# Probabilities turned by DMA in every unit, the cache copied in three stages, and a new order of work on every engine

## Chip, cores and metric

The kernel runs on one core of one Trainium2 chip. The time is in microseconds (us) of the device; lower is better. A core has five engines that each work through their own list of instructions and wait for one another by semaphores: PE (TensorE, matrix products), DVE (VectorE), ACT (ScalarE), POOL (GpSimd) and SP (SyncE, which here only issues transfers). Sixteen DMA engines carry the transfers.

## The reference

Two steps, each added to x, which is 8 batches of 128 rows of 512 columns:

```python
x = x + einsum('bsi,boi->bso', x, lora_weight[adapter_ids])        # layer 0
q, k, v = x @ Wq.T, x @ Wk.T, x @ Wv.T                              # 32 query heads, 8 key heads, D = 128
q, k = rope(rmsnorm(q)), rope(rmsnorm(k))                           # k over 8 key heads
k_all = concat(k_cache[block_table], k); v_all = concat(v_cache[block_table], v)   # 512 + 128 keys
o = softmax(where(valid, q @ k_all.T * SCALE, -1e30)) @ v_all       # 4 query heads share a key head
x = x + o @ Wo.T
```

The cache has 64 pages of 32 rows, and each batch names 16 of them.

## The kernel before, in words

The work is 64 units: key head hk = u // 8, batch b = u % 8. A unit projects q (four heads), k and v, norms and rotates them, takes four blocks of scores of 128x640, turns them into probabilities, multiplies them by the values, and multiplies the result by Wo into a sum kept per batch. For accuracy every factor is split into a high and a low part in 16 bits, and each product is three products (`three`, L1655 to L1657): high by high, high by low, low by high. The splitting of weights, keys, values, outputs and probabilities is what fills DVE, ACT and POOL.

Every engine has its order written out by hand, in a loop over i. In period i, PE takes the scores of unit i (`scores`, L1729, results in S), projects unit j = i + 1 (Q and KV), multiplies the probabilities of unit w = i - 1 by the values (`times_v`, results in O) and projects the output of unit o = i - 2 (`project_o`, Y). DVE takes the row maxima (`largest`, L1331), each of which lets PE start the next block of scores. In the first periods PE also makes the products of layer 0 for batch i + 2 (`l0_product`, L1676) and turns x (`l0_turn`).

Probabilities must be turned (transposed) ahead of the product with the values. In units 0 to 7 (NA = 8) PE does that: DVE divides them by their sums (`norm`, L1255), PE turns them in five groups of four blocks (L1661, `turn_p`), ACT takes the high part (`p_hi`, L955) and DVE the low part (`p_lo`, L1365). From unit 8 on ACT writes a high plane (`upper_plane`, L1025), DVE a low plane (`lower_plane`, L1359), in pairs of heads, with the scale made by a two-column multiply (sm, L1344) and a reciprocal (rc, L1347); and SP issues four DMA transposes a unit (`turn_upper`, L535, and `turn_lower`, L547). Their results lie in the tiles `first` and `second`, which in the first periods hold the inputs of layer 0.

The cache is read in two ways. For units 0 to 8 (NL = 9) SP loads keys page by page (`load_kt`, L419, 16 transfers a unit) and POOL gathers values by row numbers (L636). The other heads' rows are copied in the first 14 periods to a block in device memory, `cache_rows`, in the order in which units want them: one transfer a page, 14 cache rows wide (12 for one batch), L427. `COPY_SP` and `COPY_ACT` say how many groups of four pages SP and ACT issue in each period. Later units load keys and values with one transfer each (`load_k`, L436, `load_v`, L522). In the loop of SP, `load_v` stands behind the copies of its period.

Weights of a head come in ten parts of 512 columns: 0 to 3 for q, 4 and 5 for k and v, 6 to 9 for the output. Each is loaded, squared (for a scale), its high part is made by ACT (L937) and its low part by POOL in two instructions (L647 scales it, L644 subtracts); the two 16-bit rings `wh` and `wl` have twenty places. The tables `SQUARES`, `HI_ACT`, `LO_POOL`, `LO_DVE` and `LOAD_AT` say in which period relative to a head's first unit each is done; parts 4 and 5 have both high and low part two periods ahead, and the projection of k and v for the head's first unit is done one period ahead.

Of the kernel before, what the change touches and what calls it, by code (L numbers as in the profile page):

```python
# [10 lines left out]
F16 = mybir.dt.float16  # L11
# [33 lines left out]
T_BANK = (0, 1, 0, 0, 1)  # L45

NL = NB + 1  # L50
NA = 8
# [8 lines left out]
QW_DOWN = 80.0 * ONE  # L60
ROOT_EPS = float(np.sqrt(D * EPS))
# [3 lines left out]
COPY_SP = (0, 1, 1, 1, 1, 1, 1, 2, 0, 1, 1, 1, 2, 0)  # L65
COPY_ACT = (2, 2, 3, 2, 2, 3, 3, 2, 1, 0, 0, 0, 0, 0)
NGRP = NPG // 4

# [8 lines left out]
LAST_SQUARES = {3: 0, 5: 1, 9: 2}  # L77
HI_ACT = {(0, 6): (1, 0), (0, 7): (1, 0), (0, 8): (1, 1), (0, 9): (1, 1),
# [5 lines left out]
LO_DVE = {(0, 6): (1, 1), (0, 7): (1, 1), (0, 9): (1, 1)}  # L84
LO_POOL = {(0, 8): (1, 1), (1, 0): (-4, 0), (1, 1): (-4, 1), (1, 2): (-3, 0), (1, 3): (-3, 1),
# [4 lines left out]
LOAD_AT = {(1, 0): -7, (1, 1): -7, (1, 2): -6, (1, 3): -6, (1, 4): -5, (1, 5): -5,  # L90
           (1, 6): -4, (1, 7): -3, (1, 8): -3, (1, 9): -2,
           0: -10, 1: -10, 2: -9, 3: -9, 4: -8, 5: -7, 6: -6, 7: -5, 8: -5, 9: -4}


def at_period(table, period, slot=None):

    found = []
    for hk in range(NK):
        for c in range(NWC):
            own = hk == 0 or (table is LO_POOL and (hk, c) in LO_DVE)  # L100
            if not ((hk, c) in table or (c in table and not own)):
                continue
            at = table[(hk, c)] if (hk, c) in table else table[c]
            if at == (period - NB * hk if slot is None else (period - NB * hk, slot)):
                found.append((hk, c))
    return found


def copies_of(period, act=False):


    if not 0 <= period < len(COPY_SP):
        return []
    first = sum(COPY_SP[:period]) + sum(COPY_ACT[:period]) + (COPY_SP[period] if act else 0)
    return [((k // NGRP + NL) % NB, k % NGRP)
            for k in range(first, first + (COPY_ACT if act else COPY_SP)[period])]


def build(nc, x, xt, lw, wall, kv, ids_lens, table, pages, qkw, consts, iota, out):
    with ExitStack() as ctx:  # L120
# [16 lines left out]
        wh = sb("wh", [P, 2 * NWC * WC], F16)  # L137
        wl = sb("wl", [P, 2 * NWC * WC], F16)
# [5 lines left out]
        mrow = sb("mrow", [NB, NT * P], BF16)  # L144
        iot = sb("iot", [NB, NT * P], F16)
# [19 lines left out]
        pth = sb("pth", [P, 3, G * P], F16)  # L165
        ptl = sb("ptl", [P, 3, G * P], F16)
        oh = sb("oh", [P, G * P], F16)
        ol = sb("ol", [P, G * P], F16)
        ones = sb("ones", [P, P], BF16)

# [21 lines left out]
        eq = sb("eq", [P, 2, NB])  # L192
        ek = sb("ek", [P, 2, NB])
# [23 lines left out]
        kidx1 = tabb[:, 0:NT * (NL - NB)]  # L217

# [3 lines left out]
        ang = pr[:, G * (NA % 2), 0:512].rearrange("p (b f) -> p b f", b=NB)  # L222
        rnd = pr[:, G * (NA % 2) + 1, 0:512].rearrange("p (b f) -> p b f", b=NB)
# [32 lines left out]
        def hi_made(hk, c):  # L256

            g = group(c)
            first_c, size = ((0, 4), (4, 2), (6, 4))[g]
            return size * hk + c - first_c + 1  # L260
# [8 lines left out]
        def plane(a):  # L269
            return a.bitcast(F16).rearrange("p (k n) -> p k n", n=P)  # L270

        planes = tuple((plane(f[:, 0:5 * HID // 2]), plane(f[:, 5 * HID // 2:5 * HID]))
                       for f in (first, second))
# [12 lines left out]
        def totals_at(m):  # L286
            return T[:, 0, 0:2] if m < 2 else KV[:, 384:386]

        def w_total_at(hk, g):
            if hk == 0 and g < 2:  # L290
# [21 lines left out]
        c_ilf, c_tabf, c_kidx, c_kidx1, c_pos, c_ang, c_sin, c_cos = (  # L312
            sem("c_ilf"), sem("c_tabf"), sem("c_kidx"), sem("c_kidx1"), sem("c_pos"), sem("c_ang"), sem("c_sin"),
# [7 lines left out]
        w_hi, w_lo = slots("w_hi", 3), slots("w_lo", 3)  # L321
# [4 lines left out]
        a_sqk, a_vn, a_sqq, a_exp, g_kh, a_kn, a_q, a_p, a_o = (  # L326
            sem("a_sqk"), sem("a_vn"), sem("a_sqq"), sem("a_exp"), sem("g_kh"), sem("a_kn"),
# [4 lines left out]
        made_vlo, g_kc, g_var, g_rst, v_prob = (  # L332
            sem("made_vlo"), sem("g_kc"), sem("g_var"), sem("g_rst"), sem("v_prob"))
# [3 lines left out]
        v_sm, a_f1, v_f2, g_qr = sem("v_sm"), sem("a_f1"), sem("v_f2"), sem("g_qr")  # L337
# [5 lines left out]
        w_sq, p_wt, v_ws, g_wr, g_wm = (slots("w_sq", 3), slots("p_wt", 3), slots("v_ws", 3),  # L343
                                        slots("g_wr", 3), sem("g_wm"))
# [3 lines left out]
        g_vm, g_km, v_vhi = sem("g_vm"), sem("g_km"), sem("v_vhi")  # L348
# [10 lines left out]
        copy_regs = [nc.scalar.alloc_register(f"copied{j}") for j in range(12)]  # L359
# [4 lines left out]
        def place(u):  # L364

            return (u - NA) % 2

        def slot(u, g):

            return G * place(u) + g if u < NA else (G * (u - NA) + g) % RING  # L370
# [7 lines left out]
        def turned_at(u, t):  # L378

            if u == LAST:  # L380
                return S[:, t - 2, :] if t in (2, 3) else T[:, t % 2, :]
            return T[:, T_BANK[t], :]

        def p_place(parts, u, t):

            if u == LAST:
                return planes[1][parts].rearrange("p k n -> p (k n)")[:, G * P * t:G * P * (t + 1)]
            return (pth, ptl)[parts][:, (5 * u + t) % 3, :]

        def turned_part(u, t):  # L390

            return 5 * (NA if u == LAST else u) + t
# [9 lines left out]
        def taken(u):  # L402

            return 16 * ((u - NA) // 2 + 1)
# [5 lines left out]
        def load_kt(e, regs, v, t):  # L410
            if v >= 3 and t == 0:
                e.wait_ge(g_kc, v - 2)
# [11 lines left out]
        def copy_page(e, b, k, number):  # L424

            rows = slice(2 if b >= NL - NB else 4, 2 * NK)
            e.dma_start(copy[rows, b, k, :].rearrange("r (s n) -> s r n", s=16),  # L427
                        kv[rows, bass.ds(number, 1), :].rearrange("r a (s n) -> (a s) r n", s=16)
                        ).then_inc(d_copy[b], 16)

        def load_k(e, v):
            hk, b = divmod(v, NB)
            if v < NL + NB:
                e.wait_ge(d_copy[b], 16 * NPG)
            e.wait_ge(g_kc, v - 2)
# [4 lines left out]
        def l0_bank(b):  # L440
            return Y[:, :] if b <= 3 else KV[:, :]

        def w_cols(hk, c):
            n = NWC * (hk % 2) + c
            return slice(n * WC, (n + 1) * WC)
# [4 lines left out]
        def wait_products(e, hk, c):  # L450

            if hk >= 2:
                u = NB * (hk - 1) - 1
                if c < 4:
                    e.wait_ge(p_q, 4 * u + c + 1)
                elif c < 6:
                    e.wait_ge(p_kv, u + 1)
                else:
                    e.wait_ge(p_y, 4 * u + c - 6 + 1)
# [19 lines left out]
        def _(e):  # L479
# [30 lines left out]
            def copy_pages(b, t):  # L510
# [3 lines left out]
                for j in range(4):  # L514
                    copy_page(e, b, 4 * t + j, numbers[j])

            def load_v(v):
                hk, b = divmod(v, NB)
                if v < NL + NB:
                    e.wait_ge(d_copy[b], 16 * NPG)  # L520
                e.wait_ge(made_vlo, v - 2)
# [4 lines left out]
            def turn_upper(u, pair):  # L526
                if pair == 0:


                    if u == NA:  # L530
                        e.wait_ge(l_mm, NB)
                    elif u >= NA + 2:
                        e.wait_ge(p_pv, 5 * (u - 2) + 5)
                e.wait_ge(a_f1, G * (u - NA) + 2 * pair + 2)
# [5 lines left out]
            def turn_lower(u, pair):  # L540
                if pair == 0:
                    if u == NA:
                        e.wait_ge(l_mm, NB)
                    elif u >= NA + 2:
                        e.wait_ge(p_pv, 5 * (u - 2) + 5)
                e.wait_ge(v_f2, G * (u - NA) + 2 * pair + 2)
# [21 lines left out]
            load_x(0)  # L568
            e.dma_start(kwc[:, :], qkw[D:2 * D].unsqueeze(1)).then_inc(d_kwc, 16)
            for t in range(2):  # L570
                load_kt(e, kt_regs, 0, t)
# [3 lines left out]
            load_kt(e, kt_regs, 0, 2)  # L575
# [1478 lines left out]
```

## Time and profile before

| | |
|---|---|
| median of 3 runs | 1097.03 us (1094.78 to 1098.75) |
| profiled execution | 1094.0 us, span 1092.0 us |
| busy, share of the span | PE 90%, DVE 84%, POOL 79%, ACT 73% |
| granted clock of PE, mean | 0.97 |
| transfers | 505733 packets, 173.69 MB, mean 159 GB/s |

The span is the stretch that the profile's instructions fill. Busy shares are means over stages that have different limits. A group of instructions has a line of the kernel, an engine, an operation, and output and input tiles, then the number of times, busy time and mean duration; what stands behind the last stroke is how long the engine stood idle just before them, with what ended the wait.

### The profile page before, as it was taken

How to read it: one execution, taken by the hardware profiler on the slowest of the kernel's cores; microseconds unless marked ns; L12 is line 12 of the kernel's file. 1: busy time of each engine (PE TensorE's matmuls, PEld its weight loads, DVE VectorE, ACT ScalarE, POOL GpSimd, SP SyncE). 2: the span in 40 equal slices, each digit the busy share in tenths (PEclk: the TensorE clock that was granted, in tenths of full speed). 3: DMA queues.
4: the chain of work that ended last, by engine and by line, in shares of the span. 5: the costliest groups of instructions: out<-in, count | busy, mean ns of one | idle time of the engine just before them, and what ended most of it. 6: DMA issues, size and time to landing. Idle time of an engine off the chain costs nothing.

```text
span 1092.0 us, 20813 instructions
## 1 busy us (share of the span) xinstructions
PE 977.4 (90%) x5617; PEld 559.3 (51%) x5617; DVE 920.3 (84%) x1942; ACT 796.4 (73%) x2202; POOL 863.5 (79%) x1184
## 2 busy tenths in 40 slices
PE   6787997789868999989998999899998999899997
PEld 4344554455434555545554555455555555455554
DVE  6576876578868999989997999979997999899994
ACT  4364655468677888878887888878887888777873
POOL 3656567558858998889898998889888988989881
PEclk9889999899999999999999999999999999999999
DMA  8688977738897777766778677876776777757862
GB/s 256 174 230 239 246 229 221 207 106 160 179 187 137 142 154 157 138 136 142 158 140 162 128 144 157 148 145 140 154 139 139 153 158 140 130 99 133 152 140 64
DMA packets 505733, 173.69 MB, mean 159 GB/s; under 512 B 429121, under 2 KB 487762, under 8 KB 505618
## 3 DMA queue, kind: packets, MB, share of 16 engines
q1 hardware_dynamic: 482752, 149.76, 65.5%
q10 hardware_dynamic: 21714, 20.25, 6.1%
q0 software_dynamic: 1152, 2.36, 0.8%
q8 instruction: 46, 0.75, 0.3%
q14 instruction: 69, 0.57, 0.2%
HBM read 98.11 MB, written 31.86 MB: 119 GB/s over the span
## 4 chain that ended last, share of the span: by engine, by line
PE 42%; DVE 19%; issue 4%; POOL 2%; ACT 2%; DVEq 0%; POOLq 0%; ACTq 0%
PE S L1729 10%; DVE pr L1359 5%; DVE pr L1331 5%; DVE sm L1344 4%; PE Y L1655 4%; PE Y L1657 4%; PE Y L1656 4%; PE Q L1656 3%; PE Q L1655 3%; PE Q L1657 3%; PE O L1655 2%; PE O L1656 2%; PE O L1657 2%; PE T L1661 2%; POOL wl L644 2%
## 5 line engine op out<-in xcount | busy, mean ns | idle before, releaser
L1359 DVE SCALAR_TENSOR_TENSOR pr<-pr,rc,upper 128x640 f16<-128x640 f32 x220 | 235.2, 1069 | 20.5 <-ACT upper L1025 13.8
L1331 DVE CUSTOM_DVE_ANT_0 pr<-S,mask,rst 128x640 f32<-128x640 f32 x256 | 224.4, 876 | 30.8 <-PE S L1729 19.2
L1025 ACT ACTIVATE upper<-pr,rc 128x640 f16<-128x640 f32 x220 | 170.3, 820 | 75.7 <-DVE rc L1347 75.6
L1045 ACT ACTIVATE pr<-pr,nb 128x640 f32<-128x640 f32 x256 | 209.6, 819 | 17.5 <-DVE nb L1331 14.5
L1729 PE MATMUL S<-kh,qh 128*128 128x320 f16 x512 | 113.0, 303 | 41.9 <-DVE nb L1331 41.9
L754 POOL TENSOR_TENSOR m<-m 128x512 f32<-128x512 f32 x63 | 81.7, 1297 | 78.1 <-DVE m L1403 78.1
L1729 PE MATMUL S<-kl,qh 128*128 128x320 f16 x512 | 112.3, 301 | 0.9 <-POOL kl L644 0.9
L1729 PE MATMUL S<-kh,ql 128*128 128x320 f16 x512 | 112.5, 302 | 0.0
L644 POOL TENSOR_TENSOR wl<-wraw,wh 128x512 f16<-128x512 f32 x71 | 104.2, 1468 | 5.9
L1729 PEld LDWEIGHTS S<-kh,qh 128*128 128x128 f16 x512 | 45.9, 99 | 116.1 <-DVE nb L1331 71.1
L1655 PE MATMUL Q<-wh,xh 128*128 128x512 f16 x256 | 99.9, 390 | 4.1 <-issue 2.8
L1656 PE MATMUL Q<-wl,xh 128*128 128x512 f16 x256 | 100.1, 391 | 0.0
L1657 PE MATMUL Q<-wh,xl 128*128 128x512 f16 x256 | 100.1, 391 | 0.0
L1655 PE MATMUL Y<-wh,oh 128*128 128x512 f16 x252 | 96.5, 383 | 0.2 <-DVE ol L1197 0.2
L1656 PE MATMUL Y<-wl,oh 128*128 128x512 f16 x252 | 96.5, 383 | 0.0
L1657 PE MATMUL Y<-wh,ol 128*128 128x512 f16 x252 | 96.5, 383 | 0.0
L984 ACT ACTIVATE Q<-Q 128x128 f32<-128x128 f32 x256 | 67.6, 264 | 37.1 <-DVE m L1403 37.1
L1655 PE MATMUL KV<-wh,xh 128*128 128x256 f16 x256 | 72.5, 283 | 19.5 <-POOL wl L644 19.5
L785 POOL TENSOR_TENSOR pw<-var,mhalf 128x5 f32<-128x5 f32 (+1 forms) x64 | 76.0, 1188 | 5.3
L644 POOL TENSOR_TENSOR vl<-vraw,vh 128x640 f16<-128x640 f32 x56 | 78.4, 1400 | 0.0
L647 POOL TENSOR_SCALAR wraw<-wraw,sw 128x512 f32<-128x512 f32 x71 | 49.4, 696 | 35.9 <-ACT wh L937 33.5
L915 ACT ACTIVATE v_left<-vraw 128x640 bf16<-128x640 f32 x64 | 46.5, 726 | 42.5 <-DMA vraw<-in_kv,kidx 24.4
(218 smaller groups left out, 2719.4 us busy)
## 6 DMA issues: line engine op xcount, KB each, us to landing
wraw<-in_wall SPq DMA_DIRECT2D x74, 256.0 KB, 3.5
cache_rows<-in_kv ACTq DMA_DIRECT2D x80, 224.0 KB
rawk<-cache_rows SPq DMA_DIRECT2D x55, 256.0 KB
vraw<-cache_rows SPq DMA_DIRECT2D x55, 256.0 KB, 4.6
cache_rows<-in_kv SPq DMA_DIRECT2D x36, 224.0 KB
second<-in_lw SPq DMA_DIRECT2D x4, 1024.0 KB
first<-in_lw SPq DMA_DIRECT2D x3, 1024.0 KB
cache_rows<-in_kv SPq DMA_DIRECT2D x16, 192.0 KB, 3.6
```

The costliest lines, as they stand in the source:

```text
L644: return e.tensor_tensor(dst, src, hi, ALU.subtract)
L754: e.tensor_tensor(m1[:, :, :], m1[:, :, :], m2[:, :, :], ALU.add).then_inc(q_added, 1)
L785: e.tensor_tensor(pw[:, j % 2, s], var[:, j % 2, s], mhalf[:, s], ALU.pow).then_inc(g_pow, 1)
L984: made = e.activation(part, part, ACT.Square, accum_out=ssq[:, j % 2, r:r + 1])
L1025: e.activation(upper16[:, g, :], pr[:, slot(u, g), :], ACT.Copy, scale=rc[:, u % 2, g:g + 1]).then_inc(a_f1, 1)
L1045: e.activation(pr[:, slot(u, g), :], pr[:, slot(u, g), :], ACT.Exp, bias=nb[:, u % 2, g:g + 1], scale=-1.0, accum_out=sm[:, u % 2, g:g + 1 ...
L1331: e.tensor_tensor_reduce(pr[:, slot(u, g), :].rearrange("p (a n) -> p a n", a=2), S[:, :, 0:320], mask[:, u % NB, :].rearrange("p (a n) -> ...
L1359: e.scalar_tensor_tensor(out=lower16(u, g), in0=pr[:, slot(u, g), :], scalar=rc[:, u % 2, g:g + 1], in1=upper16[:, g, :], op0=ALU.mult, op ...
L1655: e.matmul(dst, lh, rh, start=first, stop=False)
L1656: e.matmul(dst, lh, rl, start=False, stop=False)
L1657: return e.matmul(dst, ll, rh, start=False, stop=last)
L1729: made = e.matmul(S[:, a, 0:320], l[:, u % 2, qs], r[:, u % 2, 320 * a:320 * a + 320], start=first, stop=last)
```

## The change

Probabilities of all units but the last are turned by DMA. They are divided, scaled and split as units 8 and later were, and the turned planes get a tile of their own (`turned`). PE's turning, `norm`, and the per-block `p_hi` and `p_lo` stay for the last unit alone. Values are split by POOL in all units. Direct loads and gathers stay for units 0 to 3 (NL = 4).

The copies are made in three stages of cache rows: rows 0 to 5 in periods 0 to 7 (16 pages a period; batches 0 to 3 without the first two rows), rows 6 to 9 in periods 8 to 23 and rows 10 to 15 in periods 24 to 39 (8 pages a period). All are issued by SP, half before the upper and lower turns of heads 2 and 3, half after.

The rings of weights have sixteen places. The squares write into a tile of their own. Low parts 0, 2, 5, 6 and 8 are made by DVE in one instruction, the others by POOL; each low part comes one period after its high part, parts 4 and 5 having their high parts three periods ahead.

The order changes: in PE's period the last product with values stands before the projection of k and v; on ACT the planes are spread and the score scale (`score_scales`) is made there; on DVE the second scale of the planes moves behind the period's end, and the weights' low part stands behind the first row maximum; on POOL values come before keys, weights before the sum of q, low keys last.

```diff
-NL = NB + 1
-NA = 8
+NL = 4
+WRING = 16
+HI_ACT = {(0, 6): 0, (0, 7): 0, (0, 8): 0, (0, 9): 0,
+          (1, 0): -5, (1, 1): -5, (1, 2): -4, (1, 3): -4, (1, 4): -3, (1, 5): -3,
+          0: -6, 1: -5, 2: -5, 3: -4, 4: -3, 5: -3, 6: -1, 7: -1, 8: 0, 9: 0}
+DVE_CHUNKS = (0, 2, 5, 6, 8)
+LO_DVE = {k: at + 1 for k, at in HI_ACT.items() if chunk(k) in DVE_CHUNKS}
+LO_POOL = {k: at + 1 for k, at in HI_ACT.items() if chunk(k) not in DVE_CHUNKS}
+STAGE_ROWS = (slice(0, 6), slice(6, 10), slice(10, 16))
+def stage_of(hk):
+    return 0 if hk < 3 else 1 if hk < 5 else 2
+def copies_of(period):
+    if 0 <= period < 8:
+        return [(0, (period + NL) % NB, t) for t in range(4)]
+    if 8 <= period < 40:
+        n = period - 8
+        return [(1 + n // 16, n % 16 // 2, 2 * (n % 2) + t) for t in range(2)]
+    return []
...
+        turned = sb("turned", [P, 4, 5 * G * P], F16)
...
         def w_cols(hk, c):
-            n = NWC * (hk % 2) + c
+            n = (NWC * hk + c) % WRING
...
 SP
+            for i in range(0, NU + 2):
+                w, early = i - 1, i < NB
+                copied = copies_of(i)
+                if NL <= i + 1 < NU:
+                    load_v(i + 1)
+                if early and i + 3 < NB:
+                    load_x(i + 3)
+                if early and 2 <= i + 1 < NB:
                     load_mask(i + 1)
+                if 0 <= w < LAST:
+                    turn_lower(w, 0)
+                if not early and i + 3 < NU:
+                    load_k(e, i + 3)
                 next_weights(i)
...
+                for part in copied[0:len(copied) // 2]:
+                    copy_pages(*part)
+                if 0 <= w < LAST:
+                    turn_upper(w, 1)
+                    turn_lower(w, 1)
+                for part in copied[len(copied) // 2:]:
+                    copy_pages(*part)
+                if early and i + 3 >= NL:
                     load_k(e, i + 3)
                 if i < LAST:
                     turn_upper(i, 0)
...
 POOL
+                kv_scales(j)
+                if nxt:
+                    keys_scaled(j)
+                if w >= 0:
+                    values_scaled(w)
+                if nxt:
+                    keys_hi(j)
+                if w >= 0:
+                    output_back(w)
+                    values_hi(w)
+                    values_lo(w)
...
+                    split_w(i)
+                    if nxt:
+                        q_sum(j)
+                        norm(j)
+                        keys_lo(j)
...
 DVE
+                if 0 <= w < LAST:
+                    scaled_recip(w, 1)
+                if real:
+                    largest(i, 0)
...
+                split_w(i)
+                if 0 <= w < LAST:
                     lower_plane(w, 2)
+                if 0 < i < NU:
                     largest(i, 1)
...
 PE
-                project_q(j)
-                if turn:
-                    turn_p(w, 0)
...
+                if o >= 0:
+                    times_v(o, 4)
+                if nxt:
+                    project_kv(j)
```

## Rows read from the trace of the kernel before

**Rows 1.** The page, first part: busy time, share, instructions of each engine.
```profile
PE 977.4 (90%) x5617; PEld 559.3 (51%) x5617; DVE 920.3 (84%) x1942; ACT 796.4 (73%) x2202; POOL 863.5 (79%) x1184
```
**Rows 2.** Busy time by stretch; the last three columns are clock, DMA share, GB/s.
```profile
0.00:36.86 36.86, 24.65 (x111) 15.40 (x111) 21.17 (x62) 16.94 (x46) 16.57 (x40) 0.91 0.78 237
36.86:231.37 194.51, 157.87 (x842) 91.06 (x843) 133.60 (x308) 103.28 (x302) 118.57 (x192) 0.92 0.77 218
...
251.11:367.70 116.59, 99.59 (x587) 56.01 (x585) 96.61 (x198) 83.53 (x233) 91.85 (x124) 0.99 0.82 164
...
606.81:726.35 119.54, 112.25 (x660) 63.80 (x658) 109.81 (x226) 97.82 (x270) 107.11 (x140) 0.99 0.75 146
...
994.89:1062.21 67.32, 66.84 (x395) 38.54 (x393) 61.68 (x137) 53.81 (x149) 56.04 (x72) 1.00 0.76 145
...
265.48:280.99 15.51, 14.12 (x83) 7.63 (x81) 13.95 (x29) 11.81 (x33) 14.65 (x20) 1.00 0.88 186
```
**Rows 3.** The chain through unit 34, which has weights: start, length, what.
```profile
636.20 0.89 DVE pr L1331
...
644.95 0.44 PE T L1661 x4
...
649.24 1.05 DVE sm L1344
...
650.46 0.89 DVE pr L1331
```
**Rows 4.** The timeline of DVE through unit 60, without weights.
```profile
1021.42 0.88 DVE L1331 CUSTOM_DVE_ANT_0 pr<-S,mask,rst 128x640 f32<-128x640 f32 x1
...
1022.26 2.54 DVE L1359 SCALAR_TENSOR_TENSOR pr<-pr,rc,upper 128x640 f16<-128x640 f32 x2
...
1026.65 0.69 DVE L1399 TENSOR_TENSOR m<-Q,tab 128x512 f32<-128x512 f32 x1 [0.44 <-PE Q L1657]
...
1034.61 0.15 DVE L1344 TENSOR_SCALAR sm<-sm 128x2 f32<-128x2 f32 x1
...
1035.02 0.88 DVE L1331 CUSTOM_DVE_ANT_0 pr<-S,mask,rst 128x640 f32<-128x640 f32 x1
```
**Rows 5.** Waits in unit 31, where the head changes: in total, times, longest.
```profile
PE KV L1655 <- POOL wl L644: 3.2, 1, 3.2
```
**Rows 6.** Waits in unit 13.
```profile
ACT v_left L915 <- DMA vraw<-cache_rows: 7.3, 1, 7.3
```
**Rows 7.** Groups of instructions by form in units 1 to 7.
```profile
L1661 PE MATMUL T<-ident,pr 128*128 128x128 f32 x140 | 22.0, 283 | 11.6 <-DVE ptl L1365 10.9 <-DVE pr L1255 0.7
...
L915 ACT ACTIVATE v_left<-vraw 128x640 bf16<-128x640 f32 x7 | 5.1, 733 | 24.4 <-DMA vraw<-in_kv,kidx 24.4
```
**Rows 8.** The timeline of PE in unit 4: the product of layer 0.
```profile
143.14 3.60 PE L1676 MATMUL KV<-first 128*128 128x512 f32 x8
```
**Rows 9.** The timeline of SP, whose rows are issues, in three stretches.
```profile
24.56 4.67 SPq L419 DMA_DIRECT2D rawk<-in_kv  x8
...
298.00 2.84 SPq L547 DMA_TRANSPOSE second<-pr  x1
...
307.34 7.20 SPq L427 DMA_DIRECT2D cache_rows<-in_kv  x8
...
637.83 1.32 SPq L535 DMA_TRANSPOSE second<-upper  x1
```
**Rows 10.** The page, third and sixth part: a queue, and issue to landing.
```profile
q10 hardware_dynamic: 21714, 20.25, 6.1%
...
first<-pr SPq DMA_TRANSPOSE x56, 3.4
```
**Rows 11.** The page, fifth part: the low parts of weights on POOL.
```profile
L644 POOL TENSOR_TENSOR wl<-wraw,wh 128x512 f16<-128x512 f32 x71 | 104.2, 1468 | 5.9
...
L647 POOL TENSOR_SCALAR wraw<-wraw,sw 128x512 f32<-128x512 f32 x71 | 49.4, 696 | 35.9 <-ACT wh L937 33.5
```
**Rows 12.** Low parts of weights on DVE in start-up: shortest, median, longest ns.
```profile
L1197 DVE SCALAR_TENSOR_TENSOR wl<-wraw,sw,wh x6: 743/747/753, 15.0 to 26.1; 128x512 f16<-128x512 f32 x6
```

More of the change, by code:

```diff
@@ new lines, in at_period, with squares_order @@
+def at_period(table, period):
+    return [(hk, c) for hk in range(NK) for c in range(NWC) if own_period(table, hk, c) == period]
+def squares_order():
+    order = [(0, 4), (0, 5), (0, 0), (0, 1), (0, 2), (0, 3)]
+    for period in range(NU):
+        order += at_period(SQUARES, period)
+    return {chunk: n for n, chunk in enumerate(order)}
+STAGE_ROWS = (slice(0, 6), slice(6, 10), slice(10, 16))
[8 more added lines that the diff above has]
+    return []
@@ L267, in stat_cols @@
             return slice(0 if m >= 2 else 1, 2 if m < NU else 1)
[L269 to L273, printed above, removed]
+        planes = tuple(tuple(turned[:, 2 * at + which, :].rearrange("p (k n) -> p k n", n=P)
+                             for which in range(2)) for at in range(2))
         def plane_tile(u, which, t):
@@ L358, in build @@
         id_reg = nc.sync.alloc_register("id")
-        copy_regs = [nc.scalar.alloc_register(f"copied{j}") for j in range(12)]
+        copy_regs = [nc.scalar.alloc_register(f"copied{j}") for j in range(4)]
         def bc(src, n):
@@ L422, in load_kt, with copy_page @@
                 ).then_inc(d_rawk[v % 3], 16)
-        def copy_page(e, b, k, number):
-            rows = slice(2 if b >= NL - NB else 4, 2 * NK)
+        def copy_page(e, stage, b, k, number):
+            rows = STAGE_ROWS[stage]
+            if stage == 0 and b < NL:
+                rows = slice(2, rows.stop)
             e.dma_start(copy[rows, b, k, :].rearrange("r (s n) -> s r n", s=16),
@@ L649, in _, with split_w @@
             w_scaled = [0]
-            def split_w(period, place):
-                for hk, c in at_period(LO_POOL, period, place):
+            def split_w(period):
+                for hk, c in at_period(LO_POOL, period):
                     e.wait_ge(w_hi[group(c)], hi_made(hk, c))
@@ L835, in _ @@
             x_back(0)
+            for t in range(1, NT):
+                gather_v(0, t)
             e.wait_ge(v_ws[0], 3)
@@ L907, in _ @@
+                if gathered and i:
+                    for t in range(2, 4):
+                        gather_v(j, t)
+                if i + 2 < NB:
+                    x_back(i + 2)
+                if (i + 2) % NB == 0 and (i + 2) // NB in range(1, NK):
+                    unit_scales((i + 2) // NB, slice(0, NB))
         @block.scalar
@@ L1512, in _ @@
             k_sum(0)
+            first_keys_lo()
             q_lo(0)
@@ L1624, in _ @@
                     k_sum(j)
+                if i == 0:
+                    for part in range(2):
+                        rope_part(1, part, 1)
+                if lb < NB:
+                    l0_add(lb)
                 if real:
@@ L1643, in _ @@
                     norm_last(3)
+                if i == 0:
+                    for part in range(2, 4):
+                        rope_part(1, part, 1)
+                    rope_part(0, 1, 1)
                 if w == LAST:
@@ L1898, in _ @@
             l0_part(1, 3)
-            for i in range(0, NA + 1):
+            for i in range(0, NU):
                 j, w, o, lb = i + 1, i - 1, i - 2, i + 2
-                turn, last = w >= 0, o >= 0
+                nxt = j < NU
                 scores(i, 0)
```

844 lines of the change are left out of this document (285 added, 559 removed), and 12 rows, old and new, of tables (HI_ACT, LO_POOL, SQUARES).

## Prediction

> **What bounds the kernel now.** I read the page's first part, then cut the span into stretches of equal work, then took one unit out of the middle and one near the end, and last the waits of the units that are longer than these. No engine is busy all the time, PE is nearest [rows 1], so the bound must be read stage by stage. The stretches of [rows 2] cut the span where the first row maximum (L1331) of units 0, 8, 9, 16 and so on starts. Start-up takes 36.86 us. Units 0 to 7, with probabilities turned by PE, take 194.51, or 24.3 each, at a DMA share of 0.77. Unit 8 takes 19.7 (231.37 to 251.11). Unit 10, shown apart, takes 15.5. Units 9 to 15, turned by DMA while copies still run, take 116.59, or 16.7 each. From then on eight units take 119.54, or 14.94. Units 58 to 62, which have no weights left to prepare, take 67.32, or 13.46, and PE is busy in 66.84 of it: there PE is the bound. The tail after 1062.21 takes 29.8 of the span of 1092.0.
>
> In the middle a unit lasts 14.26 (636.20 to 650.46) and the chain runs through DVE at its end: a two-column multiply (sm) takes 1.05 us [rows 3]. Without weights the same instruction takes 0.15, and DVE even idles 0.44 before m; the unit is 13.60 [rows 4]. So 0.66 of a unit is DVE held up while POOL splits weights. Eight units of 14.26 would be 114.1; the missing 5.4 us of each head lie mostly where the head changes: PE waits 3.2 us for POOL's wl before the KV projection [rows 5]. In units 10 to 13 it is another wait: ACT sat 7.3 us for values from the copied cache in unit 13 [rows 6], whose load stands behind the copies on SP. In units 1 to 7, ACT waited 24.4 us in all for gathered values [rows 7].
>
> **The change, part by part.** *Start-up.* POOL makes one of the high parts, ACT the first high keys, loads are reordered. The pieces are under 1 us and lie beside weights still landing; I take 0, bounds -2 to +2. Sum so far: 36.9.
>
> *Units 0 to 7.* The turning by PE goes: 20 transposes a unit, which stand in the trace as groups of four at 0.44 us [rows 3], hence 2.2 us of PE (their recorded 283 ns overlap [rows 7]). Gathers stay for units 0 to 3 only. Left on PE are the 13.6 of a bare unit, and through unit 5 the layer-0 product (eight records, 3.6 us [rows 8]) and its four transposes (0.44): 17.7; 13.6 in units 6 and 7. But the copies move wholly to SP, 16 pages in each unit, and so do the turns. SP issues eight 16 KB loads in 4.67 us [rows 9], so four in 2.3; of the old, wider copies eight took 7.20, so 3.6 a group of four. The new pieces are smaller (6 or 4 rows of cache in place of 14), so I take the lower side plus 0.4 for crowding, 2.7 a group. Four groups 10.8, four turns of 1.32 [rows 9] 5.3, inputs, mask, keys and weights about 4.3: 20.4 us of SP. DMA: a middle unit needs 0.75 x 14.94 = 11.2 us of all sixteen engines [rows 2]. Inputs of layer 0 are 1.5 MB; start-up moved 237 GB/s at a share of 0.78, 304 GB/s when full, so 5.2. Copies: the ACT queue's 21714 packets, nearly all copies of 1 KB, took 6.1% of the span [rows 10], 49 ns each; 16 pages x 16 pieces x 6 rows = 1536 packets, 4.7 us. In all 21 us in units 0 to 3, and with the share of 0.9 that I allow, 23.5 each: 94. Units 4 and 5 have a third fewer copied rows and are held by SP and PE at about 20.5: 41. Units 6 and 7 have no inputs to load: SP 17.5 each, 35. Sum 170, against 194.5. Bounds: DMA and PE perfectly fed, 155; nothing gained, 195.
>
> *Units 8 to 39, the spread copies.* Before, they took 19.7 + 116.6 + 3 x 119.55 = 495. The wait on values goes: their load is now first on SP in each unit. The wait at the head change goes too: five of ten low parts leave POOL (0.70 + 1.47 us each [rows 11], 10.9 us a head), and all are due a unit or more before use; with sixteen places no high part waits for a product still to run. DVE takes the five, 0.75 each [rows 12], 3.7 us a head. It has 0.44 us free before m in a bare unit [rows 4] and 0.66 less to lose at a unit's end where sm is short, so most is hidden, and POOL has 10.9 us less in which to hold DVE up. Without copies I therefore put a unit between 13.6 (PE) and 14.26 (as now), at 14.1. What goes the other way: SP must issue two groups of copies in these units, 5.4, beside 5.3 of turns and 2 to 3 of loads: 12.7 to 13.7 of 14.3, fitting with little air. SP's order is lower turn, keys, weights, four pages, upper turn, lower turn, four pages. The low part of the last two heads is ready on DVE at about 5.2 us of the unit (maximum 0.9, weights 0.75, low part 1.1, maximum 0.8, output 0.6, low part 1.0). A turn lands 3.4 us after issue [rows 10], 8.7 to 9.1, and PE reaches its first product with it at about 9. Landing may slip to about 10.5 before the unit is longer than 14.3, since after it come 2.9 us of products, 0.8 of scores and the maximum. DMA work rises from 11.2 to 13 or 13.6 us (512 or 768 packets more). Measured nearest: unit 10, with four 14-row pages on SP, took 15.5 at a DMA share of 0.88 [rows 2], and a turn was issued in 2.84 instead of 1.32 [rows 9]. So the bounds are 14.0 and 15.5; near their middle, since values no longer wait: 14.8, or 474.
>
> *Units 40 to 57*: 18 x 14.1 = 254 (before 268.5). Bounds 13.7 and 14.6. *Units 58 to 63 and the tail*: the same work, 97.1.
>
> Sum: 36.9 + 170 + 474 + 254 + 97 = 1032, against the span of 1092.0. The profiled execution itself took 1094.0, 2.0 more; the median of the runs is 1097.03, 3.0 above that. So 1032 + 5 = **1037**.
>
> Small moves at no cost: the score scale goes from POOL (0.35) to ACT, which idles some 2 us a unit; the value scale back is one more 0.2 us instruction on POOL, which waits for DVE's m anyway; the turned planes get tiles of their own, so turns no longer wait for layer 0. New waits: SP's key load waits for a copy issued a period or more earlier, and queued behind it are the turns; if a copy landed so late, the products would wait.
>
> **Rules weighed.** The wait of sm in rows 3 against rows 4 looks like one engine blocked, not slowed. The Trainium skill (SBUF — State Buffer, "Who interferes with whom") says that GpSimd and VectorE share one port pair as an exclusive lock, and that a VectorE instruction with two SBUF inputs contends with GpSimd's reads. The trace agrees: 1.05 against 0.15. By that rule the moved splits, which read wraw and wh, can each wait behind an instruction of POOL. The case is rival C.
>
> Turns behind copies: SP's turn took 2.84 in place of 1.32 with copies about. The Trainium skill (DMA: Bandwidth & Descriptors, "Queues, rings and completion order") says that each engine consumes one queue's descriptors in ring order and goes round robin between queues. Before, most copies came from ACT's queue; on SP's they would stand ahead of the turns. The trace agrees as far as the stretched issue shows it. The case is rival D.
>
> **The rivals.** A, as summed, 1037: chance 0.5.
>
> B, the copies are hidden: 14.1 in units 8 to 39 too, 22 us less, 1015. For it: DMA keeps spare share, and turns have 1.5 us of slack. Against: unit 10. 0.2.
>
> C, VectorE becomes the bound: each moved split costs 0.75 and a wait of up to POOL's 1.47, and low parts of probabilities already take 2.54 for two where one takes 0.88. Five splits at 1.5 a head, none hidden, raise the unit by 0.9: 15.2 beside copies, 14.8 without. 37 + 170 + 486 + 266 + 97 + 5 = 1061. Against: DVE's idle time, and POOL's relief. 0.17.
>
> D, slower: SP and its queue become the bound, turns landing behind eight copies in every unit up to 39. At 17.2 a unit (the units of 9 to 15 took 16.7 on average), and early units as before: 37 + 195 + 550 + 254 + 97 + 5 = 1138; early units as summed, 1113. It decides from 16.7 a unit on, where the spread copies eat what the rest gives. Against: the pieces are less than half as large, and what held units 10 to 13 was the value load. 0.09.
>
> E, the change doesn't do what it says: the head change still waits, for the high part on ACT or the squares, and early units stay: 1090 to 1097. 0.04.
>
> **Numbers.** Predicted 1037. The range takes in B and C and some of the bounds, 995 to 1085; it leaves out D and the two ends at which all bounds fall together (988 and 1095). About 0.3% can be told from no change. Faster: A, B, C and half of E, 0.88; the same 0.03; slower 0.09.
>
> **What would show it.** Right: no PE wait for wl at the head change; eight units from 40 on in 111 to 115; sm short in half the units; PE transposes only for m, xs and the last unit; units 0 to 3 with a DMA share of 0.9. Wrong: PE's first O product waiting for DMA in units 8 to 39 by over 1 us; SP without idle time; DVE idle nowhere and m late; ACT waiting for vraw. What would make the number wrong first is the price of a small copy on SP, which no row shows.

## The result: slower, and the profile after

The changed kernel takes 1188.31 us (median of 4, 1183.29 to 1196.61) beside 1096.22 us of the kernel before: ratio 1.0845, 95% interval 1.0775 to 1.0915. The forecast was 1037, faster; the time lies outside the range and on the other side. The profiled execution has a span of 1183.7 us.

The page of the changed kernel, its first part, a queue of the third and a row of the fifth, answers to [rows 1]:

```profile
PE 991.3 (84%) x5457; PEld 547.7 (46%) x5457; DVE 929.6 (79%) x1936; ACT 807.4 (68%) x2258; POOL 793.9 (67%) x1053
...
q1 hardware_dynamic: 549920, 181.50, 74.5%
...
L1507 PE MATMUL O<-turned,vh 128*128 128x512 f16 x315 | 134.8, 428 | 134.3 <-DMA turned<-pr 134.1
```

The queue q1 now carries nearly all packets; q10, which had 21714 of them [rows 10], has 3666 left. Every engine has a smaller share than before, and PE waited 134.1 us for one thing: the DMA transpose of the low planes, ahead of its product with the values. Where in time, the stretches say. They are cut at the first row maximum of a unit again (units 0, 8, 16, 32, 40, 48 and 56 start the rows) and answer to [rows 2]:

```profile
38.76:253.40 214.64, 147.56 (x698) 77.60 (x699) 122.77 (x274) 109.67 (x308) 120.55 (x181) 0.84 0.71 169
253.40:396.50 143.10, 119.72 (x659) 65.27 (x658) 113.00 (x231) 99.01 (x280) 95.47 (x123) 0.93 0.76 157
...
679.98:822.90 142.92, 121.02 (x660) 66.15 (x658) 110.98 (x230) 99.27 (x280) 96.06 (x124) 0.92 0.80 166
822.90:940.10 117.20, 111.96 (x662) 62.76 (x660) 112.76 (x230) 98.35 (x277) 95.92 (x122) 1.00 0.83 148
940.10:1056.10 116.00, 111.73 (x661) 62.34 (x660) 113.31 (x232) 98.38 (x277) 96.31 (x123) 1.00 0.78 141
1056.10:1155.30 99.20, 96.77 (x569) 54.68 (x566) 94.54 (x192) 77.84 (x219) 77.51 (x96) 1.00 0.71 136
```

As long as copies run the units are long: 26.8 us each in units 0 to 7, 17.8 in units 8 to 39. From unit 40 on, without copies, eight units take 117.2 and 116.0, less than the 119.5 of before. The DMA share beside the long units is only 0.71 to 0.83, so the DMA engines aren't full. Now SP, whose rows are issues (start and length), through one unit and a bit:

```profile
580.19 1.40 SPq L527 DMA_TRANSPOSE turned<-upper  x1
581.64 1.41 SPq L536 DMA_TRANSPOSE turned<-pr  x1
584.41 2.81 SPq L420 DMA_DIRECT2D cache_rows<-in_kv  x4
587.32 1.39 SPq L527 DMA_TRANSPOSE turned<-upper  x1
588.80 0.54 SPq L519 DMA_DIRECT2D vraw<-cache_rows  x1
590.29 1.34 SPq L536 DMA_TRANSPOSE turned<-pr  x1
591.72 1.27 SPq L431 DMA_DIRECT2D rawk<-cache_rows  x1
593.04 1.32 SPq L506 DMA_DIRECT2D wraw<-in_wall  x1
595.01 2.85 SPq L420 DMA_DIRECT2D cache_rows<-in_kv  x4
597.91 1.52 SPq L527 DMA_TRANSPOSE turned<-upper  x1
```

From one turn of heads 2 and 3 to the next, 580.19 to 597.91, are 17.7 us. The issues in it sum to 14.3. The gaps of 1.36 and 0.65 before the copies hold the loads of page numbers (1.02 and 0.31 us here; 0.69 is the median in units 8 to 39) and some register work, and 0.9 before 590.29 is a wait. SP has little air left. What comes of it on PE, from its timeline in the unit after:

```profile
603.11 0.58 PE L1507 MATMUL O<-turned,vh 128*128 128x512 f16 x1 [2.41 <-DMA turned<-pr]
603.49 0.63 PE L1508 MATMUL O<-turned,vh 128*128 128x512 f16 x1
603.91 0.63 PE L1509 MATMUL O<-turned,vl 128*128 128x512 f16 x1
604.34 0.63 PE L1507 MATMUL O<-turned,vh 128*128 128x512 f16 x1
604.77 0.63 PE L1508 MATMUL O<-turned,vh 128*128 128x512 f16 x1
```

PE waited 2.41 us, and after it products begin 0.43 us apart, where others of the kind lie 0.22 apart (568.00 to 568.22): PE ran at the lower of its two clocks, 1.2 GHz; from 603 to 607 us the mean granted clock is 0.58. It isn't so after every wait: the products at 568.00 follow one of 1.75 us. The four stretches of units 8 to 39 have a mean granted clock of 0.92 to 0.96 (units 0 to 7 even 0.84), the later ones 1.00. So some of PE's waits are paid for twice.

### The profile page after: what moved, and what is told of

Read it like the earlier page. It is cut to its first block and busy times, and to the rows that moved or that the text cites. A ratio compares the mean times of both kernels' runs of the same rounds, so it can differ in the third digit from the quotient of the medians.

```text
span 1183.7 us, 21098 instructions
## 1 busy us (share of the span) xinstructions
PE 991.3 (84%) x5457; PEld 547.7 (46%) x5457; DVE 929.6 (79%) x1936; ACT 807.4 (68%) x2258; POOL 793.9 (67%) x1053
## 3 DMA queue, kind: packets, MB, share of 16 engines
q10 hardware_dynamic: 3666, 2.03, 0.6%
q0 software_dynamic: 512, 1.05, 0.4%
## 5 line engine op out<-in xcount | busy, mean ns | idle before, releaser
L1264 DVE SCALAR_TENSOR_TENSOR pr<-pr,rc,upper 128x640 f16<-128x640 f32 x252 | 286.4, 1136 | 19.4 <-ACT upper L978 19.2
L1507 PE MATMUL O<-turned,vh 128*128 128x512 f16 x315 | 134.8, 428 | 134.3 <-DMA turned<-pr 134.1
L978 ACT ACTIVATE upper<-pr,rc 128x640 f16<-128x640 f32 x252 | 206.2, 819 | 0.0
L863 ACT ACTIVATE kh<-KV 128x128 f16<-128x128 f32 x64 | 17.7, 277 | 176.0 <-PE KV L1690 176.0
L1508 PE MATMUL O<-turned,vh 128*128 128x512 f16 x315 | 135.5, 430 | 0.0
L1509 PE MATMUL O<-turned,vl 128*128 128x512 f16 x315 | 135.0, 429 | 0.0
L1121 DVE TENSOR_SCALAR kve<-KV 128x2 int32<-128x2 int32 (+1 forms) x64 | 10.2, 160 | 154.0 <-PE KV L1609 148.0
L1507 PEld LDWEIGHTS O<-turned,vh 128*128 128x128 f16 x315 | 35.8, 114 | 165.8 <-issue 152.2
L631 POOL TENSOR_TENSOR vl<-vraw,vh 128x640 f16<-128x640 f32 x64 | 95.7, 1495 | 5.5
```

The source lines that it names most:

```text
L631: return e.tensor_tensor(dst, src, hi, ALU.subtract)
L863: return e.activation(dst, src, ACT.Copy)
L978: e.activation(upper16[:, g, :], pr[:, slot(u, g), :], ACT.Copy, scale=rc[:, u % 2, g:g + 1]).then_inc(a_f1, 1)
L1264: e.scalar_tensor_tensor(out=lower16(u, g), in0=pr[:, slot(u, g), :], scalar=rc[:, u % 2, g:g + 1], in1=upper16[:, g, :], op0=ALU.mult, op ...
L1507: e.matmul(dst, lh, rh, start=first, stop=False)
L1508: e.matmul(dst, lh, rl, start=False, stop=False)
```

## The experiments

Theory SP: each copy costs SP a fixed time to issue, whatever its width, and SP, which also issues all the turns, has no time left. Theory bytes: the copies' packets crowd the DMA engines or stand in front of the turns. The kernel before took 1089.56 us beside runs 1 to 4 (timed once), 1094.22 beside runs 5 to 8 and 1094.49 beside runs 9 to 12. Where a run was timed once, mind that the four times of the changed kernel lie up to 13 us apart. Ratios are to the kernel before. Runs 1, 2, 3 and 10 read other cache rows than the reference asks for and are there for their times alone.

**1. No copies in units 8 to 39** (timed once).

```diff
+def source_of(hk):
+    return hk if hk < 3 else 1 + hk % 2
...
-    if 8 <= period < 40:
-        n = period - 8
-        return [(1 + n // 16, n % 16 // 2, 2 * (n % 2) + t) for t in range(2)]
...
-                        copy[2 * hk + 1, b].rearrange("k (d r) -> d k r", r=PSZ)
+                        copy[2 * source_of(hk) + 1, b].rearrange("k (d r) -> d k r", r=PSZ)
```

> The changed kernel without the copies of stages two and three (units 8 to 39); keys and values of heads 3 to 7 are read from the copies of heads 1 and 2, so the results of these heads are other ones. Bounds what the copies cost in units 8 to 39. Both theories (SP's issue time; the copies' bytes in front of the turns): units 8 to 39 run like units 40 to 55, 14.6 us each instead of 17.8, so about 1085 us. A third theory, that the new order of work on DVE and ACT is what makes the turns late, expects little change, over 1150.

1089.01 us. Eight units take 116.0 to 116.9 us throughout from unit 16 on; units 0 to 7 are unchanged at 215.7. The copies of stages two and three cost 99 us (96 of it in units 8 to 39, 569.5 against 473.4 in the traces), and the new order isn't what makes the turns late.

**2. Eight issues a unit, one cache row wide** (timed once).

```diff
-STAGE_ROWS = (slice(0, 6), slice(6, 10), slice(10, 16))
+STAGE_ROWS = (slice(0, 6), slice(6, 7), slice(10, 11))
...                                 (source_of as in 1)
```

> As before it, but the copies of stages two and three are issued as in the changed kernel, eight a unit, each with one cache row instead of four or six. The number of issues is whole, the bytes a quarter or a sixth. Theory SP (each issue takes SP about 0.75 us whatever its width, SP has 15.5 us of work in a unit): still 16.5 to 17.8 a unit, 1150 to 1188 us. Theory bytes (the copies' packets crowd the DMA engines and stand before the turns): near the run without copies, 1085 to 1110.

1170.69 us. With a quarter to a sixth of the bytes, 82 of the 99 us stay.

**3. The bytes with two issues a unit** (timed once).

```diff
...                                 (source_of as in 1)
+                if stage:
+                    rows = STAGE_ROWS[stage]
+                    e.dma_start(copy[rows, b, 4 * t:4 * t + 4, :]..., kv[rows, 4 * t:4 * t + 4, :]...)
+                    return
                 for j in range(4):
                     copy_page(e, stage, b, 4 * t + j, numbers[j])
```

> As the run without copies, but two wide transfers a unit move as many packets of the same size as the eight copies (pages 4t to 4t+3 instead of those of the table). The bytes are whole, the issues a quarter. Theory SP: 14.6 to 15.3 a unit, 1085 to 1110 us. Theory bytes: 17 or more, 1160 to 1188 us.

1113.79 us: 25 of the 99, a little above the 1085 to 1110 of theory SP and far from the other. A transfer of four pages takes SP a median 0.60 us to issue where one of a single page takes 0.55. The run also drops the loads of page numbers (none in the trace after 248 us), so what it takes off SP is six issues and two such loads a unit together. The stretches of runs 1, 2 and 3 for units 24 to 31 stand beside each other:

```profile
494.50:611.30 116.80, 111.50 (x661) 62.49 (x659) 113.19 (x230) 98.50 (x279) 96.22 (x123) 1.00 0.81 151
```
```profile
532.09:670.82 138.73, 118.82 (x658) 64.83 (x656) 113.39 (x232) 98.64 (x280) 95.08 (x124) 0.94 0.71 134
```
```profile
499.20:625.40 126.20, 112.76 (x660) 62.98 (x658) 113.18 (x231) 98.50 (x279) 96.21 (x123) 0.99 0.93 189
```

The second moves fewer GB/s than the first and is 22 us longer; the third has the DMA engines at 0.93 and is 9 us longer. The issues, with their loads of page numbers, are the cost, the bytes a small one. The landing of the turns says the same: from issue to landing their medians in units 8 to 39 are 3.3 us (upper) and 3.7 (lower) in the changed kernel and 3.6 and 3.6 in run 1, which has no copies there.

**4. Copies behind the turns** (timed once).

```diff
-                for part in copied[0:len(copied) // 2]:
+                ahead = len(copied) // 2 if early else 0
+                for part in copied[0:ahead]:
...
-                for part in copied[len(copied) // 2:]:
+                for part in copied[ahead:]:
```

> The changed kernel whole, but in units 8 to 39 both groups of copies stand behind the turns of heads 2 and 3. SP's work in a unit stays 15.5 us, but no copy stands before the turns that PE waits for. Theory SP with order: PE's wait for the turns shrinks and SP's own 15.5 to 16 becomes the unit, 1115 to 1135 us. Theory bytes alone: little change, since as many packets are moved, 1160 to 1188.

1178.54 us. The prediction of theory SP with order was wrong here: I expected 1115 to 1135. Taking the copies out from before the turns that PE waits for gives only about 10 us, 6 of them in units 8 to 39, which is no more than runs of one kernel differ. The copies then stand before the next unit's first turn. SP waits less between 537 and 680 us (10.7 us in all instead of 23.7) and is busy for 16.0 of 17.6 us in a unit.

**5. The weights' part alone, on the kernel before** (timed four times).

```diff
-          0: (-6, 0), 1: (-5, 0), 2: (-4, 0), 3: (-3, 0), 4: (-2, 0), 5: (-2, 1),
-          6: (-1, 0), 7: (0, 0), 8: (0, 1), 9: (1, 0)}
+          0: (-6, 0), 1: (-5, 0), 2: (-5, 0), 3: (-4, 0), 4: (-3, 0), 5: (-3, 0),
+          6: (-1, 0), 7: (-1, 0), 8: (0, 0), 9: (0, 0)}
-LO_DVE = {(0, 6): (1, 1), (0, 7): (1, 1), (0, 9): (1, 1)}
+LO_DVE = {(0, 6): (1, 1), (0, 7): (1, 1), (0, 9): (1, 1),
+          0: (-5, 0), 2: (-4, 0), 5: (-2, 0), 6: (0, 0), 8: (1, 0)}
...
-           0: (-6, 1), 1: (-5, 1), 2: (-4, 1), 3: (-3, 1), 4: (-2, 0), 5: (-2, 1),
-           6: (-1, 1), 7: (0, 0), 8: (0, 1), 9: (1, 1)}
+           1: (-4, 0), 3: (-3, 0), 4: (-2, 0), 7: (0, 0), 9: (1, 0)}
...
                     largest(i, 0)
+                split_w(i, 0)
```

> The kernel before with one part of the change alone: from head 2 on the low parts of weights 0, 2, 5, 6 and 8 are made by DVE behind the first row maximum, the others by POOL, each one period after its high part, parts 4 and 5 one period earlier on ACT. Theory: this part removes the wait for wl at the head change (18.7 us down to about 14.5) and is what makes the changed kernel's copy-free heads shorter (116.0 to 117.2 instead of 119.6): 3 to 5 us less in each of six heads, 1069 to 1080 us, ratio 0.975 to 0.985. Rival: the shorter heads come from the new order on the engines, and DVE, which is full in the kernel before, gives the gain back: 0.99 to 1.01.

Ratio 0.9834 (0.9776 to 0.9892), 1077.76 us. Eight units take 116.70 instead of 119.55 (the stretch of units 16 to 23):

```profile
364.30:481.00 116.70, 110.97 (x660) 62.85 (x659) 110.11 (x231) 98.09 (x271) 98.41 (x130) 1.00 0.74 150
```

**6. Only part 4 one period earlier, nothing to DVE** (timed six times).

```diff
-          0: (-6, 0), 1: (-5, 0), 2: (-4, 0), 3: (-3, 0), 4: (-2, 0), 5: (-2, 1),
+          0: (-6, 0), 1: (-5, 0), 2: (-4, 0), 3: (-3, 0), 4: (-3, 1), 5: (-2, 0),
...
-           0: (-6, 1), 1: (-5, 1), 2: (-4, 1), 3: (-3, 1), 4: (-2, 0), 5: (-2, 1),
+           0: (-6, 1), 1: (-5, 1), 2: (-4, 1), 3: (-3, 0), 4: (-3, 1), 5: (-2, 0),
```

> The kernel before with two entries of its tables changed from head 2 on: weight part 4 has its high part and POOL its low part one period earlier (with part 3), part 5 moves to the first place of its period. Nothing goes to DVE. If the wait at the head change is only a matter of when POOL starts, most of the 4.4 us goes and some 1 comes back where POOL has two parts: 1075 to 1080, ratio 0.98 to 0.985. If POOL has too much work in these periods, it stays within 0.5%.

Ratio 0.9841 (0.9797 to 0.9885), 1079.23 us, and 116.7 us a head as well. These two runs can't be told apart in time: for the head's wait it is enough that POOL begins earlier, and dividing the work between VectorE and GpSimd added nothing that can be seen in the sum. They come to it by different ways: the units of a head are 14.3 us with three of 15.1 in run 6 and lie between 12.9 and 15.4 in run 5.

**7. One wide later stage** (timed once).

```diff
-STAGE_ROWS = (slice(0, 6), slice(6, 10), slice(10, 16))
+STAGE_ROWS = (slice(0, 6), slice(6, 16))
...
-    if 8 <= period < 40:
+    if 8 <= period < 28:
         n = period - 8
-        return [(1 + n // 16, n % 16 // 2, 2 * (n % 2) + t) for t in range(2)]
+        return [(1, k // 4, k % 4) for k in range(8 * n // 5, 8 * (n + 1) // 5)]
```

> The changed kernel with two stages instead of three: rows 6 to 15 are copied in one transfer a page, 6.4 pages a period in periods 8 to 27, none after. As many bytes, half the issues. Theory SP (about 0.75 us an issue whatever its width plus the loads of page numbers): SP 8.6 + 5.6 = 14.2 us a unit in units 8 to 27, so 15 to 16 there, and 14.6 in units 28 to 39: 1188 - 570 + 20 x 15.6 + 12 x 14.6 = 1105. Theory bytes: units 8 to 27 at 18 to 19 because the packets of a unit rise from 512 or 768 to 1024: 1150 to 1165.

1148.36 us, 40 less than the changed kernel, but 43 more than theory SP said. Units 28 to 39 fall to 14.2 to 15.7 us as expected; units 8 to 27 stay near 17.5, where theory SP said 15 to 16, and their DMA share was 0.93. The time lies just below the range of theory bytes. This run doesn't decide between SP and bytes by itself; run 11 does for the larger part.

**8. All rows in periods 0 to 7** (timed once).

```diff
-STAGE_ROWS = (slice(0, 6), slice(6, 10), slice(10, 16))
+STAGE_ROWS = (slice(0, 16),)
```

> The changed kernel with all rows copied at once in periods 0 to 7, 16 or 14 rows wide, all by SP, none after. The issues of periods 0 to 7 are the same in number, the bytes of each 2.7 to 4 times. Theory SP: units 0 to 7 stay near 27 us as long as the DMA engines keep up (28 us of DMA work in units 0 to 3 by 49 ns a packet), so 215 to 235 for the eight, and units 8 to 39 at 14.6: 1188 - 570 + 467 + 0 to 20 = 1085 to 1105. Theory bytes: units 0 to 7 at 33 or more, over 1130.

1123.48 us: units 0 to 7 in 246.8 at a DMA share of 0.94, units 16 to 39 in about 117 for each eight. Between the two expectations: in units 1 to 4, at 33 to 36 us and a DMA share of 0.98, the bytes were the likely bound; no run changed them there alone. What the width does to an issue, the groups of the copy's line show for 12 and 14 rows (the kernel before), one row (run 2, whose group also holds 128 copies of 4 and 6 rows), 4 and 6 rows (changed kernel) and 14 and 16 rows (this run); shortest, median and longest ns:

```profile
L427 SPq DMA_DIRECT2D cache_rows<-in_kv x52: 120/559/2285, 71.4 to 314.0; - x52
```
```profile
L424 SPq DMA_DIRECT2D cache_rows<-in_kv x384: 492/502/1711, 50.2 to 804.4; - x192
```
```profile
L420 SPq DMA_DIRECT2D cache_rows<-in_kv x384: 553/554/1567, 51.4 to 818.7; - x192
```
```profile
L417 SPq DMA_DIRECT2D cache_rows<-in_kv x128: 553/554/2000, 51.2 to 283.9; - x128
```

**9. Half of the copies issued by ACT** (timed four times).

```diff
 SP
-                for part in copied[0:len(copied) // 2]:
-                    copy_pages(*part)
 ACT
...                                 (pages_of: the pages of parts[0:len(parts) // 2])
+                for at in pages_of[0:len(pages_of) // 2]:
+                    copy_page(e, *at)
                 if nxt:
                     q_squares(j)
...
+                for at in pages_of[len(pages_of) // 2:]:
+                    copy_page(e, *at)
                 if nxt:
                     q_hi(j)
```

> The changed kernel with half of the copies in every stage issued by ACT instead of SP; SP's other half stands behind the turns. Bytes, widths and stages are the changed kernel's. Theory SP: SP falls from 15.5 us of work a unit to 12.1 in units 8 to 39 and from 23.7 to about 17 in units 0 to 7, while ACT rises from 12.3 to 15.3 of work: units 8 to 39 at 15.3 to 16, units 0 to 7 at 21 to 23, 1065 to 1090 us. Theory bytes: no fewer packets, no change, 1170 to 1190.

Ratio to the kernel before 0.9769 (0.9718 to 0.9819), 1068.84 us: 119 us less than the changed kernel, with every byte, width, stage and period of the copies as it has them. Units 0 to 7 and units 8 to 39:

```profile
39.18:218.50 179.32, 141.89 (x700) 76.02 (x701) 122.59 (x275) 109.66 (x308) 119.39 (x182) 0.90 0.86 202
```
```profile
218.50:702.50 484.00, 450.88 (x2633) 251.82 (x2631) 452.35 (x921) 394.84 (x1114) 384.39 (x489) 0.99 0.96 189
```

The DMA share rises to 0.96 while the units get shorter. SP's remaining copies stand behind the turns here, as in run 4, which gave about 10 us at most.

**10. Four issues a unit in units 0 to 7** (timed once): run 1, with each group of four pages one transfer.

```diff
-                for j in range(4):
-                    copy_page(e, stage, b, 4 * t + j, numbers[j])
+                e.dma_start(copy[rows, b, 4 * t:4 * t + 4, :]..., kv[rows, 4 * t:4 * t + 4, :]...)
```

> As the run without copies in units 8 to 39, and in periods 0 to 7 each group of four pages is one transfer of as many packets (pages 4t to 4t+3 instead of those of the table), 4 issues a unit instead of 16. Bounds what the issues cost in units 0 to 7. Theory SP: SP's work there falls from 23.8 us a unit to 14 or 15, and the eight units from 215 us to 165 to 180: 1040 to 1055 us. Rival, DMA engines and the long waits for turns are the bound there: over 1075.

1033.04 us, below the 1040 to 1055 that theory SP gave; units 0 to 7 take 168.1 instead of 215.7, at a DMA share of 0.93. The loads of page numbers are gone with the issues, as in run 3:

```profile
38.09:206.20 168.11, 136.95 (x700) 74.67 (x701) 122.11 (x274) 109.48 (x308) 120.93 (x182) 0.93 0.93 223
```

**11. Run 7 with half on ACT** (timed once): the edits of runs 7 and 9 together.

> The changed kernel with the two stages of the run with wide copies (6.4 pages a period in periods 8 to 27) and, as in the run with half of the copies on ACT, half of stage one's groups and one group of each pair later on ACT. Theory SP: units 28 to 39 at 14.6, units 8 to 27 at 15.5 to 16.5, units 0 to 7 at 21 to 23: 1055 to 1080 us. If the DMA engines bound units 8 to 27 (their share was 0.92 with wide copies), these stay at 17 or more: over 1090.

1068.99 us, 79 less than run 7 with the same bytes; 39 of it in units 0 to 7 and 35 in units 8 to 27. These fall to 15.8 on average (252.6 us for units 8 to 23), and units 28 to 39 take 14.6. So of what held units 8 to 27 near 17.5 in run 7, SP was the larger part, 1.7 us a unit.

**12. Run 6 with the values' load first on SP** (timed four times), the kernel before otherwise.

```diff
             for i in range(NA, NU + 2):
+                if NL <= i + 1 < NU:
+                    load_v(i + 1)
...
-                if NL <= i + 1 < NU:
-                    load_v(i + 1)
```

> The kernel before with weight part 4 one period earlier (as run before) and one line moved: SP's load of the values stands first in its period instead of behind the copies. Takes the wait of units 10 to 13 away (17.5 and 21.7 us in units 12 and 13): 8 to 14 us less than with part 4 alone, 1066 to 1072 us, ratio 0.972 to 0.978. If the load only waited for crowded DMA engines, no gain over 0.984.

Ratio 0.9816 (0.9756 to 0.9877), 1072.79 us. Units 11, 12 and 13 take 14.3, 14.3 and 18.2 instead of 16.3, 17.5 and 21.7 in run 6, 9 us less for units 8 to 15. The ratio misses the 0.972 to 0.978 expected. In the total its interval overlaps that of run 6, so the gain is seen in the trace, not proved by the times.

## Why the prediction was wrong

The step that failed is SP's sum: "The new pieces are smaller (6 or 4 rows of cache in place of 14), so I take the lower side plus 0.4 for crowding, 2.7 a group", and with it "12.7 to 13.7 of 14.3, fitting with little air". The price hardly followed the width: a median of 0.554 us an issue at 4 and 6 rows as at 14 and 16, 0.49 at one row. A group takes 2.85 us of issues and, in units 8 to 39, a median 0.69 for its page numbers: 3.5 instead of 2.7. The turns cost a median 1.46 (upper) and 1.39 (lower) where I had 1.32. The loads of keys, values and weights came to 2.6 us a unit, inside my 2 to 3. Summed from SP's records, its work in units 8 to 39 is 15.5 us a unit: issues 13.3, page numbers 1.4, register work 0.9. That is more than the 14.3 it was to fit in. Three splits of the copies had tripled their issues (384 instead of 132), and all moved to the engine that must also issue 4 turns a unit; SP alone had 52 before. The lower side came from the 16 KB loads of keys (2.3 us for four in [rows 9]), another kind of transfer; the copies themselves, 3.6 a group in the same rows and 0.559 an issue in the trace of before, were the nearer ones. The prediction had named this price as what would make the number wrong first.

The second term that failed is what SP waits, which the sum put at nothing: the unit is 17.8, 2.3 more than SP's work. SP's work laid beside the unit, us a unit in units 8 to 39, shows where SP sets it (the last three columns) and where it has room:

| | run 1 | run 3 | run 9 | run 2 | changed | run 4 |
|---|---|---|---|---|---|---|
| SP's work | 8.8 | 11.2 | 12.8 | 15.0 | 15.5 | 16.0 |
| unit | 14.8 | 15.6 | 15.1 | 17.4 | 17.8 | 17.6 |

Rival D named this outcome with a chance of 0.09 and in the right place (SP as the bound, up to unit 39). It said 17.2 a unit and 1138 us; measured were 17.8 and 1188, 20 of the missing 50 in units 0 to 7, which it left as before. Half of its mechanism isn't borne out: the turns landed no later than without copies (3.3 and 3.7 against 3.6 and 3.6 us in run 1), and all the bytes in the same queue cost 25 us (run 3). SP's time did the rest.

Term by term, against the span: start-up 36.9 forecast, 38.8 measured. Units 0 to 7 170 and 214.6. Units 8 to 39 474 and 569.5. Units 40 to 57 254 and 262.6. The rest 97.1 and 98.2. The misses sum to 151.7 us, of which 140 lie where SP issues copies.

Of the signs named beforehand, those of a wrong prediction came: PE waited for turns in units 8 to 39 for 68.1 us in 24 waits, and SP had little idle time. Of those of a right one, PE's wait for `wl` at the head change and the long sm of 1.05 us were gone, but eight units from 40 on took 117.2 and 116.0 where 111 to 115 was forecast, and the DMA share in units 0 to 3 was 0.76, not 0.9.

- *Turning by PE goes, 17.7 us of PE left in units 0 to 5*: the turning went, but SP's 20.4 was about 24 (25.2 in units 0 to 3, 22.5 in units 4 to 7), and it bound. With four issues instead of sixteen (run 10) the eight units take 168.1, and with half on ACT (run 9) 179.3, beside my 170.
- *The spread copies, 14.8 a unit*: run 9 has 484.0 for the 32 units, 15.1 each. The forecast was near for an SP that has room.
- *The wait at the head change goes*: right; 116 to 117 a head from unit 40 on and in run 5. But my 14.1 a unit was too low; 14.5 to 14.6 was measured. The new order isn't needed to explain that: runs 5 and 6, in the old order, have the same 116.7 for eight units. Only the last units, without weights, are longer with the new order, 14.0 instead of 13.6.
- *DVE takes five splits, mostly hidden* (against rival C): they took 0.75 each as costed. But DVE didn't get air: in units 48 to 55 it is busy 113.3 of 116.0 us, more than PE (111.7), where before it was 109.6 of 119.7. By the Trainium skill (SBUF — State Buffer, "Who interferes with whom") an instruction of DVE can wait behind one of POOL. The moved splits show hardly any of it, a median of 749 ns and 1069 the longest from unit 8 on. The hold-up of sm did go (median 0.16 us instead of 1.05), but part of it came back elsewhere, at k's sum, which reads the same in both kernels:

```profile
L1437 DVE CUSTOM_DVE_ANT_0 k<-k,pw x16: 694/697/699, 735.8 to 960.8; 128x128 f32<-128x128 f32 x16
```
```profile
L1342 DVE CUSTOM_DVE_ANT_0 k<-k,pw x16: 1177/1246/1247, 833.0 to 1051.7; 128x128 f32<-128x128 f32 x16
```

  The first is of before, the second of the changed kernel. In all 16 units from 40 to 55 it now starts while POOL makes the low keys (`kl`) and ends about 0.15 us behind them; before, it started beside POOL's high keys. No run moved this instruction alone.
- *The bytes*: 25 us for units 8 to 39 (run 3). With DMA shares of 0.96 on average (run 9) a unit took 15.1 against 14.8 without copies. By the Trainium skill (DMA: Bandwidth & Descriptors, "Queues, rings and completion order") turns would wait behind the copies in SP's queue; here their landing, 3.3 and 3.7 us, shows no such wait, and run 3 bounds it together with the bytes at 25 us. In run 3, with the DMA engines nearer full, the turns land in 4.3 and 3.9 us and their issues take SP 7.3 us a unit, where run 1 has 6.2.
- *Not foreseen*: PE's waits lower its clock, which makes the time lost on SP larger. In units 8 to 39 PE is busy 475.7 us at a mean clock of 0.94, and 449.9 at 0.99 in run 1 with the same products. So by estimate at most 26 of the 96 us there are products at the lower clock.
- The chances of A, B, C and half of E sum to 0.89, not 0.88.

Left open: why the unit is 2.3 us longer than SP's work. In them SP waits for planes of ACT and DVE and for PE to free the turned tile, which themselves wait for SP. Run 4 shows that this isn't mended by the order alone.

## What to carry to other kernels

Count the issues as well as the bytes when a transfer is cut into stages: here each took SP about 0.55 us from 4 to 16 rows, and an engine that "only issues" has a sum like any other, to be made from rows of the same kind of transfer. Add what it waits for in its order; a sum just below the unit doesn't mean that it fits. Where one engine issues all that the critical path waits for, give part of the rest to another one: half of the copies on ACT turned 8% slower into 2.3% faster. And look at the small parts of a large change one by one: five table entries for three weight parts (run 6) held 1.6% of gain by themselves.

## What was not expected of the hardware

A device-memory-to-device-memory copy of a page took SP 0.554 us to issue from 4 to 16 rows (medians 0.553 to 0.559) and 0.49 at one row; one transfer of four pages took 0.60 (run 3). A load of four page numbers into registers took SP 0.30 to 1.08 us: a median of 1.02 in the 40 directly behind a lower turn, about 0.30 behind copies and weights. After a wait of 2.4 us PE's products came 0.43 us apart instead of 0.22. The same instruction on DVE, k's sum, took 0.70 us beside POOL's cast of the high keys and 1.25 beside its low keys.
